# A state-space decoder layer: the first rows of running sums in two transfers, and the load of x behind the rows of step 1

## The chip, the cores and the metric

One core of a Trainium2 chip runs the whole layer in one launch. The metric is the device time of that launch in microseconds (us), the median of several runs. Five engines work side by side, each through its own list of instructions: TensorE (PE, matmuls), VectorE (DVE), ScalarE (ACT), GpSimd (POOL) and SyncE (SP, which here issues the DMA transfers). They wait for one another only by semaphores. A transfer is queued when SP issues it; the 16 DMA engines of the core carry it out.

## The reference, cut to what matters

The input x is 16 batches x 128 positions x 256 values, kept in float32. The layer is x = norm(x + mixer(x)), then x = norm(x + attention(x, ctx)), then x = norm(x + experts(x)). The change concerns only the mixer, a gated state-space mixer with 32 heads of 16 values and a state of 128. With proj = x @ W_in.T it splits into val, gate, B, C and dt, val passes a causal convolution over four positions and a silu, and per chunk of positions it computes

```python
dt = softplus(dt + dt_bias)
ld = dt * -exp(A_log)
cum = cumsum(ld)
diff = where(mask, cum[l] - cum[m], -inf)
M = (C @ B.T) * exp(diff)
Y = M @ val + C @ h * exp(cum) + D * val
out = (Y * silu(gate)) @ W_out.T
```

The reference carries a state h from chunk to chunk of 32 positions. The kernel takes all 128 positions of a batch as one chunk, for which the state at its start is zero, so that only M @ val and D * val are left.

## The kernel before, in words

`build` runs three stages one after the other: `mixer`, `attention` and `experts`. Only `mixer` is touched.

**Steps.** The mixer has 16 steps n (STEPS). The heads are cut into 4 groups of 8 heads (GROUPS), the batches into 4 blocks of 4 batches (TB blocks of NB batches, 512 tokens). Step n works on token block n % 4 and head group n // 4. Within a step there are 8 slots s, one for each head of the group. For each slot PE projects B and C (`pair`, line 789, three fp16 passes that stand for an fp32 product), ACT and DVE bring the two out of the PSUM banks as a high and a low fp16 part (`evac_b`, `evac_c` on ACT, lines 443 and 447; `low_b`, `low_c` on DVE, lines 651 and 655), PE multiplies them (`scores`, line 831), and DVE multiplies the scores by the decay exp(diff) (`weigh`, line 623). Four slots later PE applies the result to the values (`outputs`, line 843).

**The decays.** diff needs the running sums of the head along both axes. The sums lie once with tokens on the free axis, one row per head and batch (`dz`). For one axis they are turned by PE (`turn_sums`) into `cum_t`. For the other one, the rows have to stand on all 128 partitions: SP stores the sums to a scratch tensor in HBM (`store_sums`, line 192) and reads them back, broadcast to all partitions, into the tile `rows` (named cum_rows in the trace) by `load_rows` (line 197). One such load brings four heads of a group (a "quad") for four batches, 8 KB that is written to 128 partitions, 1 MB in all. `rows` has two slots, par 0 and 1, for slots 0 to 3 and 4 to 7 of a step; its layout in a partition is batch, head, position, so a batch's four heads are 2 KB in one piece. POOL then runs `exponents(n, par)`: for each of the four heads a subtraction of `cum_t` (line 286) and a causal select (line 297, `causal`), the select of head q one place behind the subtraction of head q + 1. ACT follows with `decays(n, e)`, an exp in place (line 437), and DVE with `weigh(n, e)`.

**SP's order.** SP works through its list in order: x block 0, the weight chunks, `store_sums(0, 1)` for block 0 when the sums are there, then (after the store has landed) `load_rows(0, 0, 0)`, x blocks 1 to 3 (`load_x`, tile xt_raw, shown as q_rows, 512 KB each), then a wait for `rows0`, `load_rows(0, 1, 1)`, the small dskip and the weights `wo`, a wait for the sums of all blocks, `store_sums(1, TB)`, the 2 MB of x for the residual (tile `acc`, line 212), the small `expo`, a wait for the store, and then a loop over groups with the rows of later steps. `next_rows(n, par)` waits until the slot of `rows` is free: semaphore `mixed` counts the `weigh` of DVE, and for n = 1, par = 0 it needs `weigh(0, 3)`. Each group's body has the rows of its four steps and the reload of the nine weight chunks for the next group.

**The first step.** It has an order of its own on every engine, written out by hand. PE runs `pair(0,0)` to `pair(0,3)` with `scores(0,0)` and `scores(0,1)` in between, then `step_widths(1)` and `step_widths(2)` (line 802: the dt projection of x blocks 1 and 2, each of which waits for its block of x), `scores(0,2)`, which waits for `weigh(0,0)` by the semaphore `mixed`, `turn_values(0)`, `step_widths(3)`, and then the pairs 4 to 7, each with the scores of the slot before. ACT splits the weight chunks into high parts (`hi_part`), runs `decays(0,0)` to `decays(0,2)` behind `hi_part(0,8)`, then, after PE's `step_widths(3)`, the `softplus` of blocks 1 to 3 (lines 413 to 417). DVE follows with `step_sizes`, `rates` (line 588) and three running sums (`sums`, line 569), between which `low_b(0,4)` and `low_c(0,4)` stand; `scores(0,4)` needs these. POOL runs the low parts of chunks 2 to 5 (`lo_part`, line 267), `exponents(0, 0)` with `lo_part(0, 6)` before its last select, `exponents(0, 1)` with two more low parts, `split_x(1)`, the low part of wo, `exponents(1, 0)`, `exponents(1, 1)` and so on.

**The residual.** `acc` is first used by DVE's `add_out(1, 0)` (line 646) in step 1, which waits for `in_x` at 32 (x and expo). POOL waits for the same semaphore much later, before the norm.

Of the kernel before, what the change touches and what calls it, by code (L numbers as in the profile page):

```python
# [84 lines left out]
def mixer(nc, io, acc, moments, heads):  # L85

    with ExitStack() as ctx:
# [88 lines left out]
        def _(sp):  # L176
# [23 lines left out]
            sp.wait_ge(sem("dt_cum"), 1)  # L200
            store_sums(0, 1)
            sp.wait_ge(sem("cum_out"), 16)
            load_rows(0, 0, 0)
            for t in range(1, TB):
                load_x(t)
            sp.wait_ge(sem("rows0"), 16)
# [2 lines left out]
            sp.dma_start(wo, io["wo"]).then_inc(sem("in_wo"), 16)  # L209
            sp.wait_ge(sem("dt_cum"), TB)  # L210
            store_sums(1, TB)
            sp.dma_start(acc[:], io["x"]).then_inc(sem("in_x"), 16)
            sp.dma_start(expo[:], io["expo"]).then_inc(sem("in_x"), 16)
            sp.wait_ge(sem("cum_out"), 32)

            def next_rows(n, par):
                tb, grp = n % TB, n // TB

                sp.wait_ge(sem("mixed"), 8 * n + 4 * par + 1)
                load_rows(tb, grp * 2 + par, par)  # L220
# [6 lines left out]
                        src = ctx_parts[32 * half + 8 * kv:32 * half + 8 * kv + 8, part]  # L227
                        sp.dma_start(k_rows[r:r + 8, 8 * half:8 * half + 8, :, kv, :].rearrange("d b t n -> d (b t) n"), src).then_inc(sem("k_load"), 16)

            with sp.Fori(0, GROUPS - 1) as g:  # L230
                next_rows(g * TB + 1, 0)
                next_rows(g * TB + 1, 1)
                for c in range(CHUNKS):

                    sp.wait_ge(sem("w_ready"), CHUNKS * g + c + 1)
                    sp.dma_start(w_raw[:, c].rearrange("p k n -> p (k n)"),
                                 io["w_in"][bass.ds(g + 1, 1), :, c].rearrange("g p k n -> (g p) (k n)")).then_inc(chunk_loaded(c), 16)
                with sp.Fori(2, TB + 1) as t:
                    next_rows(g * TB + t, 0)
                    next_rows(g * TB + t, 1)  # L240
            n = STEPS - TB
            sp.wait_ge(sem("w_ready"), CHUNKS * GROUPS)
            sp.dma_start(ctx_t, io["ctx_t"]).then_inc(sem("in_ctx"), 16)
# [19 lines left out]
        def _(pool):  # L263
# [16 lines left out]
            def exponents(n, par, chunks={}):  # L280

                tb, quad = n % TB, (n // TB) * 2 + par
                pool.wait_ge(sem(f"rows{par}"), 16 * n + 16)
                for q in range(4):
                    own = cum_t[:, :, bass.ds(tb * H + 4 * quad + q, 1)].broadcast_to([P, NB, L])
                    nc.gpsimd.tensor_tensor(rows[:, par, :, q], rows[:, par, :, q], own, ALU.subtract).then_inc(sem("since"), 1)  # L286
                    if q > 0:
                        causal(n, par, q - 1)
                    if q in chunks:
                        lo_part(0, chunks[q])  # L290
                causal(n, par, 3)
# [1446 lines left out]
```

## Time and profile before

| what | value |
|---|---|
| three runs | 777.16, 778.05, 782.04 us; median 778.05 |
| profiled execution, its own time | 778.42 us |
| its span | 776.5 us |
| granted TensorE clock, mean over the span | 0.982 |
| first step and what is ahead of it | up to about 46 us |
| steps 1 to 15 of the mixer | from about 46 to about 545 us |

Times in the rows are from the start of the span. A timeline row gives the start, the duration of an instruction or of several merged, the engine, the line of kernel.py, what is written and read, the count, and in brackets how long the engine was idle before it and what released it. PEld is the weight load of TensorE. Starts and ends of neighbours on PE, ACT and DVE overlap by about a tenth of a microsecond or more, since they are pipelined. SP's rows are the issues of transfers; the landing of a transfer shows in who waited for it.

### The profile page before, as it was taken

The page shows a single profiled execution, that of the slowest core. Times are in us where ns is not written, and L with a number is a line of the kernel's source. Part 1 is how long each engine was busy: PE and PEld are TensorE (multiplying, and loading weights), DVE is VectorE, ACT ScalarE, POOL GpSimd, SP SyncE. Part 2 cuts the span into 40 slices and gives each one's busy share as a digit, 9 for nine tenths or more (in the row PEclk, how much of TensorE's full clock was granted, in tenths as well). Part 3 has the DMA queues.
Part 4 walks back from the last instruction along what each step waited for, and adds up shares of the span by engine and source line. Part 5 has one row for each costly group of instructions (what it writes and reads, how often), then busy time and mean ns, then how long its engine had stood idle before and what let it go on. Part 6 is the DMA issues. An engine that isn't in the chain of part 4 may idle for free. (4 is left out here: it accounts for less than half of the span.)

```text
span 776.5 us, 17302 instructions
## 1 busy us (share of the span) xinstructions
PE 736.3 (95%) x5918; PEld 407.9 (53%) x5918; DVE 577.2 (74%) x1128; ACT 454.2 (58%) x889; POOL 352.1 (45%) x411
## 2 busy tenths in 40 slices
PE   8899999999999999999999999999689999679996
PEld 4456556565555655556555565656224443244554
DVE  5676867768676686776868679786688899838776
ACT  7754448644355754544575544646267788638775
POOL 3867535635433593333649645563023311230343
PEclk9999999999999999999999999999689999979999
DMA  6694231335224232642213324220050000000001
GB/s 208 190 232 152 55 69 47 102 54 175 62 48 107 49 59 54 175 106 49 62 54 83 106 62 92 56 55 1 15 193 23 15 23 23 14 2 1 28 28 55
DMA packets 34282, 57.91 MB, mean 75 GB/s; under 512 B 7040, under 2 KB 11904, under 8 KB 33664
## 3 DMA queue, kind: packets, MB, share of 16 engines
q1 hardware_dynamic: 33664, 57.08, 28.1%
q8 instruction: 23, 0.38, 0.2%
q10 hardware_dynamic: 576, 0.31, 0.1%
q14 instruction: 19, 0.16, 0.1%
HBM read 54.10 MB, written 2.36 MB: 73 GB/s over the span
## 5 line engine op out<-in xcount | busy, mean ns | idle before, releaser
L286 POOL TENSOR_TENSOR cum_rows<-cum_rows,cum_t 128x512 f32<-128x512 f32 x128 | 136.1, 1073 | 194.6 <-DMA cum_rows<-cum_scratch 194.6
L789 PE MATMUL pring<-xt_hi,w_hi 128*128 (+1 forms) x576 | 171.6, 380 | 0.0
L789 PE MATMUL pring<-xt_lo,w_hi 128*128 (+1 forms) x576 | 171.3, 379 | 0.0
L789 PE MATMUL pring<-xt_hi,w_lo 128*128 (+1 forms) x576 | 171.3, 379 | 0.0
L651 DVE TENSOR_TENSOR bt<-pring,bt 128x512 f16<-128x512 f32 x128 | 88.1, 688 | 71.5 <-ACT bt L443 71.5
L443 ACT CAST bt<-pring 128x512 f16<-128x512 f32 x128 | 74.6, 583 | 111.5 <-PE pring L789 111.3
L655 DVE TENSOR_TENSOR ct<-pring,ct 128x512 f16<-128x512 f32 x128 | 88.2, 689 | 53.8 <-ACT ct L447 53.5
L831 PEld LDWEIGHTS pscore<-ct,bt 128*128 128x128 f16 x1536 | 96.0, 98 | 33.8 <-issue 6.2
L831 PE MATMUL pscore<-ct,bt 128*128 128x128 f16 x1536 | 106.6, 219 | 2.8 <-issue 1.9
L447 ACT CAST ct<-pring 128x512 f16<-128x512 f32 x128 | 74.8, 585 | 52.4 <-PE pring L789 52.4
L1131 DVE TENSOR_REDUCE mx<-bank_at 128x4 f32<-128x512 f32 x128 | 83.5, 689 | 14.9 <-PE bank_at L1207 14.0
L789 PEld LDWEIGHTS pring<-xt_lo,w_hi 128*128 128x128 f16 x576 | 56.4, 98 | 68.0
L789 PEld LDWEIGHTS pring<-xt_hi,w_lo 128*128 128x128 f16 x576 | 56.4, 98 | 68.0
L623 DVE TENSOR_TENSOR mt<-pscore,cum_rows 128x512 f32<-128x512 f32 x128 | 87.1, 681 | 1.3 <-ACT cum_rows L437 1.3
L437 ACT ACTIVATE cum_rows<-cum_rows 128x512 f32<-128x512 f32 x128 | 81.2, 634 | 2.3 <-POOL cum_rows L297 2.3
L297 POOL TENSOR_SCALAR_AFFINE_SELECT cum_rows<-cum_rows 128x512 f32<-128x512 f32 x128 | 81.2, 646 | 0.0
L1093 ACT ACTIVATE probs<-bank_at 128x512 f32<-128x512 f32 x128 | 68.3, 597 | 16.7 <-PE bank_at L1216 15.1
L789 PEld LDWEIGHTS pring<-xt_hi,w_hi 128*128 128x128 f16 x576 | 50.5, 98 | 41.3 <-issue 6.5
L1046 POOL TENSOR_TENSOR acc<-acc,att 128x128 f32<-128x128 f32 (+1 forms) x32 | 14.6, 456 | 86.4 <-DVE att L1144 86.4
L1207 PE MATMUL bank_at<-k_rows,q_rows 128*128 128x512 f16 x128 | 48.4, 412 | 5.5 <-DVE mx L1131 4.0
L267 POOL TENSOR_TENSOR w_lo<-w_raw,w_hi 128x512 f16<-128x512 f32 x34 | 41.5, 1240 | 26.0 <-ACT w_raw L409 26.0
L1446 ACT ACTIVATE act_s<-bank_ex,weight 128x128 f32<-128x128 f32 x128 | 36.9, 378 | 9.2 <-PE bank_ex L1609 7.2
(153 smaller groups left out, 957.4 us busy)
## 6 DMA issues: line engine op xcount, KB each, us to landing
cum_rows<-cum_scratch SPq DMA_DIRECT2D x32, 1024.0 KB, 8.0
w_raw<-in_w_in SPq DMA_DIRECT2D x35, 256.0 KB, 6.7
q_rows<-in_xt SPq DMA_DIRECT2D x4, 512.0 KB, 11.0
acc<-in_x SPq DMA_DIRECT2D x1, 2048.0 KB, 8.5
vals<-in_vals SPq DMA_DIRECT2D x16, 128.0 KB, 2.0
out<-acc SPq DMA_DIRECT2D x8, 256.0 KB, 2.1
w_raw_e<-in_w_up SPq DMA_DIRECT2D x1, 1024.0 KB, 4.9
w_raw_e<-in_w_gate SPq DMA_DIRECT2D x1, 1024.0 KB, 6.9
```

The source lines that it names most:

```text
L286: nc.gpsimd.tensor_tensor(rows[:, par, :, q], rows[:, par, :, q], own, ALU.subtract).then_inc(sem("since"), 1)
L297: nc.gpsimd.affine_select(rows[:, par, :, q], rows[:, par, :, q], [[0, NB], [1, L]], ALU.is_ge, never, base=0, channel_multiplier=-1).then ...
L437: nc.scalar.activation(rows[:, par, :, e % 4], rows[:, par, :, e % 4], ACT.Exp).then_inc(sem("decay_exp"), 1)
L443: nc.scalar.copy(bt[:, s % 2, 0], bank[f"B{s}"][:]).then_inc(sem("b_hi"), 1)
L447: nc.scalar.copy(ct[:, s % 2, 0], bank[f"C{s}"][:]).then_inc(sem("c_hi"), 1)
L623: nc.vector.tensor_tensor(mt[:, par, s % 4].rearrange("p (b n) -> p b n", b=NB), pscore[(s + 1) % 2][:].rearrange("p (b n) -> p b n", b=NB ...
L651: nc.vector.tensor_tensor(bt[:, s % 2, 1], bank[f"B{s}"][:], bt[:, s % 2, 0], ALU.subtract).then_inc(sem("b_evac"), 1)
L655: nc.vector.tensor_tensor(ct[:, s % 2, 1], bank[f"C{s}"][:], ct[:, s % 2, 0], ALU.subtract).then_inc(sem("c_evac"), 1)
L789: mm = nc.tensor.matmul(bank[name][:], w[:, c, k, cols], x[:, k, bass.ds(n % TB, 1), :].rearrange("p o n -> p (o n)"), start=(i == 0), sto ...
L831: mm = nc.tensor.matmul(pscore[(s + 1) % 2][:, cols], bt[:, s % 2, pb, cols], ct[:, s % 2, pc, cols], start=(i == 0), stop=(i == 2))
L1093: nc.scalar.activation(probs[:, i], ring_bank("scores", 8 * b + i)[:], ACT.Exp, scale=float(8.0 ** -0.5)).then_inc(sem("probs"), 1)
L1131: nc.vector.tensor_reduce(mx[:, slot, :, i], banks[i % len(banks)][:].rearrange("p (k n) -> p k n", k=4), AX.X, ALU.max).then_inc(sem("max ...
```

## The change

The one broadcast of four heads for step 0, slot 0, becomes two broadcasts of two heads each, on the same queue one behind the other. The first raises a new semaphore, `rows_first`, the second `rows0`, which the whole one raised before. POOL waits for `rows_first` before its first subtraction and for `rows0` before its third. SP still waits for `rows0` before it issues the rows for slot 1. The load of x into `acc` and that of `expo` are moved from behind the second store of sums to behind `next_rows(1, 0)`. For that the body of the loop over groups is made a function, `load_group`, which is called once for group 0 and in the loop for groups 1 and 2.

```diff
--- before.py
+++ after.py
@@ -200,7 +200,10 @@
             sp.wait_ge(sem("dt_cum"), 1)
             store_sums(0, 1)
             sp.wait_ge(sem("cum_out"), 16)
-            load_rows(0, 0, 0)
+            for i, done in enumerate(("rows_first", "rows0")):
+                q = slice(2 * i, 2 * i + 2)
+                sp.dma_start(rows[:, 0, :, q].rearrange("p b q n -> p b (q n)"),
+                             cum_d[0].rearrange("(b h) n -> b h n", h=H)[:, q, :].rearrange("b q n -> b (q n)").partition_broadcast(P)).then_inc(sem(done), 16)
             for t in range(1, TB):
                 load_x(t)
             sp.wait_ge(sem("rows0"), 16)
@@ -209,8 +212,6 @@
             sp.dma_start(wo, io["wo"]).then_inc(sem("in_wo"), 16)
             sp.wait_ge(sem("dt_cum"), TB)
             store_sums(1, TB)
-            sp.dma_start(acc[:], io["x"]).then_inc(sem("in_x"), 16)
-            sp.dma_start(expo[:], io["expo"]).then_inc(sem("in_x"), 16)
             sp.wait_ge(sem("cum_out"), 32)
 
             def next_rows(n, par):
@@ -227,8 +228,8 @@
                         src = ctx_parts[32 * half + 8 * kv:32 * half + 8 * kv + 8, part]
                         sp.dma_start(k_rows[r:r + 8, 8 * half:8 * half + 8, :, kv, :].rearrange("d b t n -> d (b t) n"), src).then_inc(sem("k_load"), 16)
 
-            with sp.Fori(0, GROUPS - 1) as g:
-                next_rows(g * TB + 1, 0)
+            def load_group(g):
+
                 next_rows(g * TB + 1, 1)
                 for c in range(CHUNKS):
 
@@ -238,6 +239,14 @@
                 with sp.Fori(2, TB + 1) as t:
                     next_rows(g * TB + t, 0)
                     next_rows(g * TB + t, 1)
+
+            next_rows(1, 0)
+            sp.dma_start(acc[:], io["x"]).then_inc(sem("in_x"), 16)
+            sp.dma_start(expo[:], io["expo"]).then_inc(sem("in_x"), 16)
+            load_group(0)
+            with sp.Fori(1, GROUPS - 1) as g:
+                next_rows(g * TB + 1, 0)
+                load_group(g)
             n = STEPS - TB
             sp.wait_ge(sem("w_ready"), CHUNKS * GROUPS)
             sp.dma_start(ctx_t, io["ctx_t"]).then_inc(sem("in_ctx"), 16)
@@ -280,8 +289,11 @@
             def exponents(n, par, chunks={}):
 
                 tb, quad = n % TB, (n // TB) * 2 + par
-                pool.wait_ge(sem(f"rows{par}"), 16 * n + 16)
+                first = isinstance(n, int) and n + par == 0
+                pool.wait_ge(sem("rows_first" if first else f"rows{par}"), 16 * n + 16)
                 for q in range(4):
+                    if first and q == 2:
+                        pool.wait_ge(sem("rows0"), 16)
                     own = cum_t[:, :, bass.ds(tb * H + 4 * quad + q, 1)].broadcast_to([P, NB, L])
                     nc.gpsimd.tensor_tensor(rows[:, par, :, q], rows[:, par, :, q], own, ALU.subtract).then_inc(sem("since"), 1)
                     if q > 0:
```

## Rows read from the trace of the kernel before

**Rows 1.** Page, part 1: busy us, share of the span and instructions of each engine.

```profile
...
PE 736.3 (95%) x5918; PEld 407.9 (53%) x5918; DVE 577.2 (74%) x1128; ACT 454.2 (58%) x889; POOL 352.1 (45%) x411
...
```

**Rows 2.** Windows view, core 0: busy us by engine, granted clock, DMA share, GB/s.

```profile
...
60.00:545.00 485.00, 481.70 (x4256) 283.07 (x4253) 359.04 (x584) 258.64 (x458) 257.74 (x295) 1.00 0.31 76
...
```

**Rows 3.** Timeline of TensorE: start us, us, engine line op out<-in xcount [idle before <-releaser].

```profile
...
24.64 0.64 PE L802 MATMUL py<-q_rows,wdt 128*32 128x128 f32 x16 [1.30 <-DMA q_rows<-in_xt]
26.12 0.83 PE L831 MATMUL pscore<-ct,bt 128*128 128x128 f16 x12 [0.83 <-DVE mt L623]
...
27.32 0.64 PE L802 MATMUL py<-q_rows,wdt 128*32 128x128 f32 x16
...
35.24 0.83 PE L831 MATMUL pscore<-ct,bt 128*128 128x128 f16 x12 [1.32 <-issue]
...
57.30 0.69 PEld L831 LDWEIGHTS pscore<-ct,bt 128*128 128x128 f16 x12 [0.46 <-issue]
...
```

**Rows 4.** Timeline of ScalarE, 20 to 30 us.

```profile
...
24.56 0.63 ACT L437 ACTIVATE cum_rows<-cum_rows 128x512 f32<-128x512 f32 x1
...
27.16 0.63 ACT L437 ACTIVATE cum_rows<-cum_rows 128x512 f32<-128x512 f32 x1 [0.97 <-POOL cum_rows L297]
28.03 0.58 ACT L413 ACTIVATE q_rows<-py,dtb 128x384 f32<-128x384 f32 x1 [0.24 <-PE py L802]
...
```

**Rows 5.** Timeline of VectorE, 20 to 62 us.

```profile
...
25.28 0.69 DVE L623 TENSOR_TENSOR mt<-pscore,cum_rows 128x512 f32<-128x512 f32 x1 [0.93 <-ACT cum_rows L437]
...
31.04 1.51 DVE L588 SCALAR_TENSOR_TENSOR q_rows<-q_rows,rate 128x384 f32<-128x384 f32 x1 [1.28 <-ACT q_rows L417]
...
34.48 0.66 DVE L655 TENSOR_TENSOR ct<-pring,ct 128x512 f16<-128x512 f32 x1
...
55.09 1.53 DVE L682 SCALAR_TENSOR_TENSOR val_t<-th_val,conv_h 128x512 f32<-128x512 f32 x1
...
60.56 1.27 DVE L646 TENSOR_TENSOR acc<-pring,acc 128x512 f32 x2
...
```

**Rows 6.** Timeline of GpSimd, 18 to 57 us.

```profile
...
18.06 1.16 POOL L267 TENSOR_TENSOR w_lo<-w_raw,w_hi 128x512 f16<-128x512 f32 x1 [0.85 <-ACT w_raw L409]
21.28 2.05 POOL L286 TENSOR_TENSOR cum_rows<-cum_rows,cum_t 128x512 f32<-128x512 f32 x2 [2.06 <-DMA cum_rows<-cum_scratch]
23.29 0.64 POOL L297 TENSOR_SCALAR_AFFINE_SELECT cum_rows<-cum_rows 128x512 f32<-128x512 f32 x1
...
30.09 2.05 POOL L286 TENSOR_TENSOR cum_rows<-cum_rows,cum_t 128x512 f32<-128x512 f32 x2 [1.24 <-DMA cum_rows<-cum_scratch]
...
50.36 2.06 POOL L286 TENSOR_TENSOR cum_rows<-cum_rows,cum_t 128x512 f32<-128x512 f32 x2 [5.65 <-DMA cum_rows<-cum_scratch]
...
55.03 1.04 POOL L286 TENSOR_TENSOR cum_rows<-cum_rows,cum_t 128x512 f32<-128x512 f32 x1
...
```

**Rows 7.** Source view of line 682: duration ns min/median/max, first and last start.

```profile
...
L682 DVE SCALAR_TENSOR_TENSOR val_t<-th_val,conv_h x16: 676/682/1533, 15.2 to 514.6; 128x512 f32<-128x512 f32 x16
...
```

**Rows 8.** Timeline of the DMA issues on SyncE, 10 to 49 us.

```profile
...
10.22 0.35 SPq L192 DMA_DIRECT2D cum_scratch<-q_rows  x1
11.77 0.39 SPq L197 DMA_DIRECT2D cum_rows<-cum_scratch  x1
...
21.16 0.39 SPq L197 DMA_DIRECT2D cum_rows<-cum_scratch  x1
...
36.15 1.53 SPq L212 DMA_DIRECT2D acc<-in_x  x1
...
39.09 9.58 SPq L197 DMA_DIRECT2D cum_rows<-cum_scratch  x2
...
```

**Rows 9.** Windows view, 12 to 22 us, columns as in rows 2.

```profile
...
12.00:20.00 8.00, 8.00 (x57) 4.39 (x55) 5.86 (x10) 6.95 (x14) 3.48 (x3) 1.00 0.68 138
20.00:22.00 2.00, 2.00 (x14) 0.94 (x12) 0.69 (x1) 1.67 (x5) 0.72 (x1) 1.00 0.99 385
...
```

**Rows 10.** Page, part 6: DMA issues, KB each, median us to landing.

```profile
...
cum_rows<-cum_scratch SPq DMA_DIRECT2D x32, 1024.0 KB, 8.0
...
```

## The prediction

> **What bounds the kernel now.** I read the page's busy table first. TensorE (PE) is busy for 736.3 of 776.5 us [rows 1]; the other engines are far below. The windows view then says where the missing 40 us are not: from 60 to 545 us, the whole steady part of the mixer, PE is busy for 481.7 of 485 us [rows 2]. The change touches only what runs before 60 us, so it can win only what PE waits there, and what it wins or loses is carried to the end as a constant shift, since behind it PE has no slack to absorb it. The span is 776.5 us and the profiled execution took 778.42 us; the sum below is made against the latter, which lies 0.4 us over the median 778.05 of the three runs.
>
> The PE timeline of the first step has these waits [rows 3]: 1.30 us at 24.64 for the third block of x (`step_widths(2)`), 0.83 us at 26.12 for `weigh(0,0)`, 1.32 us at 35.24 before `scores(0,4)`, and in step 1 a gap of 0.46 us at 57.30 before `scores(1,1)`. Together 3.9 us, 0.5% of the kernel: no better order of these transfers can win more. For each I asked who is late, in the timelines of the other engines.
>
> - 26.12: PE waits for `weigh(0,0)` on DVE (25.28), and DVE waited 0.93 us for ACT [rows 5]. ACT ran `decays(0,0)` at 24.56, directly behind `hi_part(0,8)`, with no idle time before it [rows 4]. Its input from POOL, the first causal select, was ready at 23.29 + 0.64 = 23.93 [rows 6]. So ACT's queue is late here, by 0.6 us, not POOL and not the rows.
> - 35.24: `scores(0,4)` needs `low_c(0,4)`, which DVE ran at 34.48 to 35.14. DVE is busy back to `rates` at 31.04, which waited 1.28 us for ACT's logarithm and then itself took 1.51 us [rows 5]. ACT's part of that chain starts at 28.03, on PE's `step_widths(3)` at 27.32 [rows 3, 4]. That block of PE stands behind `scores(0,2)`, so behind the first point.
> - 57.30: `scores(1,1)` waits for the DVE chain of step 1, in which `val_silu` at 55.09 took 1.53 us; the median of its 16 executions is 0.68 [rows 5, 7].
>
> **Part 1, the first rows in two halves.** Now the whole megabyte is issued at 11.77, and has landed when SP issues the next one at 21.16, 9.4 us later [rows 8]. POOL finished `lo_part(0,5)` at 18.06 + 1.16 = 19.22, idled 2.06 us and began `exponents(0,0)` at 21.28 [rows 6]. With halves, the first lands at about 11.77 + 4.7 = 16.5, if bytes set the time; the extra issue costs SP 0.4 us (11.77 to 12.21) and only pushes the issue of x, which queues behind the rows anyway. POOL then starts at 19.22, 2.06 us earlier. It does two subtractions (2.05) and one select (0.64) and reaches the new wait for the second half at 21.9; the second half, landing as the megabyte did, is there at 21.2. Behind that new wait stand the third subtraction and all the rest of POOL's program, `lo_part(0,6)` first; none waits. `exponents(0,0)` ends 2.06 us earlier.
>
> Who profits? `decays(0,0)`: nobody, since ACT gets to it at 24.56 whatever POOL does. `decays(0,2)` at 27.16 waited 0.97 us for POOL and now comes about 1.4 us earlier, but ACT's next item, at 28.03, waits for PE's `step_widths(3)` [rows 4], which is unmoved. On POOL, the next item is `exponents(0,1)`, which already waited 1.24 us for its rows and began at 30.09 [rows 6]; those rows are issued only when `rows0` is complete, 21.16 as before, so POOL stands idle 3.3 us instead of 1.24. PE's two waits at 24.64 and 26.12 stay: the third block of x is queued behind the same bytes. I take 0 for part 1.
>
> Bounds for its unknown, the landing of the second half. The trace has no broadcast in 1 KB pieces; the old one is 512 pieces of 2 KB, the new ones 1,024 of 1 KB. Between 12 and 20 us, with the rows in front of the queue, the DMA engines moved 138 GB/s at a share of 0.68; between 20 and 22, with x on them, 385 GB/s at 0.99 [rows 9]. So a broadcast out of 8 KB of memory is slow already, and not by bytes through the engines. If each piece costs the same time whatever its size, the second half lands 8 us later, at 29.2. At the other end the halves go as fast as x: then it could land at up to 5 us earlier, and the third block of x with it; PE would win back its 1.30 us at 24.64 but still wait for ACT until about 26.1, so below nothing is worth 0. I take bytes as the measure, since both broadcast and x pieces are far larger than what the small transfers of this kernel use, and because the limit looks like one of the source, which is the same. Delays up to 0.84 us are free (PE's second wait covers a later x); above that each microsecond costs PE one.
>
> One rule of the Trainium skill speaks against the split. "DMA: Bandwidth & Descriptors", section Bandwidth, says to batch into transfers of 1 MiB or more, and its section on the anatomy of a DMA gives a fixed part of about 2.0 us for each. Where two transfers are queued one behind the other the trace shows otherwise: three transfers of 512 KB each follow one another at 385 GB/s.
>
> **Part 2, x behind the rows of step 1.** Now x (2 MB) is issued at 36.15 and the rows of step 1, first half, at 39.09, behind it [rows 8]; POOL idled 5.65 us and began at 50.36 [rows 6]. Afterwards these rows are the first in the queue. Their issue still waits for the store of the sums, so 39.09 at the latest; at the median of 8.0 us from issue to landing [rows 10] they are there at 47.1, and POOL starts 3.3 us earlier. `exponents(1,0)` is four subtractions of 1.04 and four selects of 0.64, 6.7 us, and ends at 53.8 instead of 57.1 or later.
>
> PE does not wait for POOL in step 1, so the direct gain is 0. An indirect one is in the rows: `val_silu` began at 55.09 while POOL's subtraction of 55.03 + 1.04 ran, and ended at 56.62, 0.55 after that one's end [rows 5, 6]. The same stands at 31.04, where `rates` ended 0.41 us after POOL's pair of 30.09 + 2.05. Such an operation, with both inputs in SBUF, seems held until POOL lets go. With POOL done at 53.8, `val_silu` takes 0.68 [rows 7], the chain loses 0.85 us, and PE's gap of 0.46 at 57.30 goes. Bounds: 0 if the rows land after 48.4 (then POOL still runs at 55.09), and 0.85, all that `val_silu` loses. I take the gap, 0.5. The Trainium skill has this as a rule, "SBUF — State Buffer", Who interferes with whom: VectorE and GpSimd share one pair of ports, and the second to issue waits for the whole instruction of the first; the trace agrees, with 1.53 against 0.68 us.
>
> What is late next: x itself. It now lands behind a megabyte more, at 47.1 + 8.5 = 55.6 at the latest, and its first use is `add_out(1,0)` at 60.56 [rows 5]: covered by 5 us; without cover each microsecond would be PE's, through the ring banks. The second rows of step 1 are issued when `weigh(1,-1)` is done, about 48.3, and find 2 MB ahead of them; but the sum of bytes is the same, the queue only starts its big transfer some 2 to 3 us later, so they land 1 to 3 us later than now; their first use is `decays(1,4)`, two slots of the step behind `add_out(1,0)`. The weights of group 1, which are queued next, are used three steps later. The loop body taken out for group 0 issues the same DMAs; I cost it at nothing, since SP only waits there.
>
> **Sum.** 778.42 + 0 - 0.5 = 777.9; from the median, 777.6.
>
> **Rivals.**
> 1. *The second half lands late.* For: the broadcast runs at 138 GB/s, far from the 385 of x, and half of the source addresses serve each half. Against: the engines' share of 0.68 leaves room for more pieces. It decides from 0.84 us of delay on; then x's third block holds PE at 24.64 one for one, and the rows for `exponents(0,1)`, issued when the second half is there, follow. At 4 us: 777.6 + 3.2 = 780.8. At 8 us: 784.8. Slower than before.
> 2. *Each transfer pays its fixed time in series.* The smallest bound from the rows is the 64 KB store of sums, issued at 10.22 and landed at 11.77, 1.55 us [rows 8]. A delay of 1.55 us, less 0.84, gives 777.6 + 0.7 = 778.3. Against it stand the x blocks at full rate. With the page's 2.0 us, which no run here shows, an estimate would be 778.8.
> 3. *POOL's new phase frees `rates`.* `rates` at 31.04 lost about 1 us to POOL's pair begun at 30.09. If the rows of `exponents(0,1)` land only a little later, or POOL's second subtraction starts behind the DVE operation, that microsecond goes, and PE's 1.32 us at 35.24 shrinks by it: 777.6 - 1.0 = 776.6. For: only about 0.1 us decide who goes first (31.04 against 30.09 + 1.04). Against: nothing in the change moves it on purpose.
> 4. *Nothing of it reaches PE*, part 2's half microsecond either, as the rows land after 48.4: 778.1. This is also the case in which the change does what it says and is without use.
>
> **Chances.** Forecast 0.40, rival 4 0.20, rival 3 0.17, rival 1 0.15 (most of it below 781), rival 2 0.08. A measurement of this kernel can tell about 1% (7.8 us) from no change. Faster by more is nearly excluded, since PE waits only 3.9 us where the change acts: 0.01. Slower by more needs rival 1 at its upper end and something besides: 0.02. The rest, 0.97, is no change that can be told. The range is 775.8 to 780.8: below, rival 3 with 0.8 us for the spread of the runs; above, rival 1 at 4 us.
>
> **What would show it.** Right: POOL's `exponents(0,0)` begins near 19.2 and its wait before `exponents(0,1)` grows from 1.24 to about 3.3 us; `decays(0,0)` still at about 24.5 and `scores(0,2)` at about 26.1; `exponents(1,0)` begins near 47; `val_silu` of step 1 takes 0.68 and the gap at 57.30 is gone; PE's instructions from step 2 on are 0.5 us earlier. Wrong: a second wait of POOL inside `exponents(0,0)`, SP's next rows issued well behind 22, `step_widths(2)` later than 24.64 (rival 1 or 2); `rates` at 0.5 us instead of 1.51 (rival 3); `add_out(1,0)` waiting for x.

## The result and the profile after

The change makes the kernel slower by 0.6%: the changed one has a median of 781.45 us (22 runs), the one before 776.88 us (22 runs beside them), ratio 1.0061 with a 95% interval of 1.0045 to 1.0076. The forecast was 777.6 us, and its range ended at 780.8. Ratios and intervals here and below leave out slow executions, those over 1.5% above the fastest of their kernel; only the padded changed kernel further down had any, two of twelve.

The two profiled executions hardly show this as a sum: their spans are 776.7 us after and 776.5 before. The stage that the change touches does. The last `low_y` of the mixer began at 545.16 us before and at 549.75 after, 4.6 us later, which is about the difference of the medians. What took it back in this one execution lies behind the mixer, where the clock is granted differently from execution to execution: between 650 and 700 us TensorE had 0.90 of full speed before and 0.97 after. So all that follows is read at marks inside the mixer. They carry a few tenths of spread of their own: TensorE began its last matmuls ahead of x block 1, where the change had not yet reached it, at 22.48 us after and at 22.18 before.

First SyncE's issues, which answer to [rows 8]:

```profile
...
10.73 0.35 SPq L192 DMA_DIRECT2D cum_scratch<-q_rows  x1
12.29 0.94 SPq L205 DMA_DIRECT2D cum_rows<-cum_scratch  x2
13.26 5.28 SPq L181 DMA_DIRECT2D q_rows<-in_xt  x3
26.96 0.39 SPq L197 DMA_DIRECT2D cum_rows<-cum_scratch  x1
...
41.28 0.40 SPq L192 DMA_DIRECT2D cum_scratch<-q_rows  x1
44.31 0.39 SPq L197 DMA_DIRECT2D cum_rows<-cum_scratch  x1
44.74 0.51 SPq L244 DMA_DIRECT2D acc<-in_x  x1
...
```

The two halves are issued at 12.29, and the next rows, which wait for the second half, at 26.96: 14.7 us, where the whole megabyte took 9.4. TensorE's timeline, against [rows 3]:

```profile
...
28.20 1.08 PE L814 MATMUL py<-q_rows,wdt 128*32 128x128 f32 x16 [5.12 <-DMA q_rows<-in_xt]
30.31 1.08 PE L814 MATMUL py<-q_rows,wdt 128*32 128x128 f32 x16 [1.03 <-DMA q_rows<-in_xt]
31.33 1.46 PE L843 MATMUL pscore<-ct,bt 128*128 128x128 f16 x12
...
33.36 0.64 PE L814 MATMUL py<-q_rows,wdt 128*32 128x128 f32 x16
...
40.81 0.83 PE L843 MATMUL pscore<-ct,bt 128*128 128x128 f16 x12 [0.85 <-issue]
```

TensorE waits 5.12 us for x block 1, which stands in the queue behind both halves and for which its matmuls had not waited before; `step_widths(2)` comes 5.7 us later and `scores(0,2)` 5.2 us. After the wait it also runs slowly for a while: `scores(0,2)` takes 1.46 us instead of 0.83. The windows view has the clock; its last three columns are the granted clock as a share of full speed, the busy share of the DMA engines, and GB/s:

```profile
...
12.00:20.00 8.00, 7.32 (x49) 3.79 (x48) 6.23 (x11) 7.02 (x15) 3.60 (x4) 1.00 0.66 91
20.00:22.00 2.00, 2.00 (x17) 1.11 (x15) 0.69 (x1) 1.67 (x4) 1.75 (x2) 1.00 0.82 127
20.00:27.00 7.00, 3.08 (x21) 1.41 (x18) 2.77 (x4) 5.16 (x10) 2.65 (x3) 0.95 0.81 174
27.00:32.00 5.00, 2.77 (x39) 1.87 (x40) 0.69 (x1) 1.26 (x2) 4.95 (x6) 0.50 0.97 272
...
```

From 27 to 32 us the granted clock is 0.50, the lower of the two levels, 1.2 GHz. It fell shortly after 26 us, while TensorE stood still, and was back by about 33. And the engines moved 91 GB/s from 12 to 20 us, against 138 before, and 127 instead of 385 from 20 to 22 [rows 9].

GpSimd, against [rows 6]:

```profile
...
20.25 2.05 POOL L298 TENSOR_TENSOR cum_rows<-cum_rows,cum_t 128x512 f32<-128x512 f32 x2 [0.72 <-DMA cum_rows<-cum_scratch]
...
27.01 1.05 POOL L298 TENSOR_TENSOR cum_rows<-cum_rows,cum_t 128x512 f32<-128x512 f32 x1 [4.11 <-DMA cum_rows<-cum_scratch]
...
35.48 2.23 POOL L298 TENSOR_TENSOR cum_rows<-cum_rows,cum_t 128x512 f32<-128x512 f32 x2 [3.51 <-DMA cum_rows<-cum_scratch]
...
```

The first half lands at 20.25, one microsecond before the whole did, and GpSimd begins that much sooner; then it waits 4.11 us inside `exponents(0,0)` for the second half, and 3.51 for the rows of `exponents(0,1)`. ScalarE follows:

```profile
...
24.87 0.62 ACT L449 ACTIVATE cum_rows<-cum_rows 128x512 f32<-128x512 f32 x1
28.68 0.63 ACT L449 ACTIVATE cum_rows<-cum_rows 128x512 f32<-128x512 f32 x1 [3.19 <-POOL cum_rows L309]
30.28 0.63 ACT L449 ACTIVATE cum_rows<-cum_rows 128x512 f32<-128x512 f32 x1 [0.97 <-POOL cum_rows L309]
34.07 0.58 ACT L425 ACTIVATE q_rows<-py,dtb 128x384 f32<-128x384 f32 x1 [3.15 <-PE py L814]
...
```

`decays(0,0)` stays where it was, behind `hi_part(0,8)`, as forecast; `decays(0,1)` now waits 3.19 us.

### The profile page after: what moved, and what is told of

Its sections match the earlier page's. It is cut to its first block and busy times, and to the rows that moved or that the text cites. A ratio compares the mean times of both kernels' runs of the same rounds, so it can differ in the third digit from the quotient of the medians.

```text
span 776.7 us, 17261 instructions
## 1 busy us (share of the span) xinstructions
PE 732.9 (94%) x5910; PEld 406.3 (52%) x5918; DVE 575.4 (74%) x1128; ACT 453.8 (58%) x889; POOL 352.4 (45%) x411
```

## The experiments

The theories changed on the way; the expectations show how. Marks in the mixer for all of them stand in a table at the end of this section.

**The two parts alone.** The first has the split, with x for the residual left where it was:

```diff
             store_sums(1, TB)
+            sp.dma_start(acc[:], io["x"]).then_inc(sem("in_x"), 16)
+            sp.dma_start(expo[:], io["expo"]).then_inc(sem("in_x"), 16)
...
             next_rows(1, 0)
-            sp.dma_start(acc[:], io["x"]).then_inc(sem("in_x"), 16)
-            sp.dma_start(expo[:], io["expo"]).then_inc(sem("in_x"), 16)
             load_group(0)
```

> Only the split of the first rows; x for the residual stays where the kernel before has it. If the split alone makes the loss: the second half lands some 6 us later than the whole megabyte did, SP issues the next rows near 27 instead of 21.2, TensorE waits about 5 us for the x block of step_widths(1), and the time is 4 to 6 us above the kernel before, ratio about 1.006. If moving x makes it: 778 or so, ratio 1.000.

Measured: 782.17 us beside 776.96, ratio 1.0064 (1.0042 to 1.0085), the whole loss. The second half landed at 27.24.

The second has the move alone:

```diff
-            for i, done in enumerate(("rows_first", "rows0")):
-                q = slice(2 * i, 2 * i + 2)
-                sp.dma_start(...).then_inc(sem(done), 16)
+            load_rows(0, 0, 0)
...
-                pool.wait_ge(sem("rows_first" if first else f"rows{par}"), 16 * n + 16)
+                pool.wait_ge(sem(f"rows{par}"), 16 * n + 16)
```

> Only the move of x; the first rows come in one transfer. My prediction for this part alone: exponents(1,0) begins near 47 instead of 50.4, val_silu of step 1 takes 0.7 us, TensorE's gap before scores(1,1) goes, and the time is 0.5 us below the kernel before, ratio 0.999. The rival, that x or the second rows of step 1 come too late: add_out(1,0) waits, ratio above 1.002.

Measured: 776.49 us beside 776.96, ratio 0.999 (0.9967 to 1.0013). The size is the forecast one, but the interval holds 1 as well. The mixer's end mark moved by 0.5 us, to 544.64. The timelines of GpSimd and VectorE in step 1:

```profile
...
49.68 2.05 POOL L292 TENSOR_TENSOR cum_rows<-cum_rows,cum_t 128x512 f32<-128x512 f32 x2 [4.68 <-DMA cum_rows<-cum_scratch]
...
```

```profile
...
54.99 0.94 DVE L688 SCALAR_TENSOR_TENSOR val_t<-th_val,conv_h 128x512 f32<-128x512 f32 x1
...
56.45 1.10 DVE L645 TENSOR_TENSOR y_parts<-skip,y_parts 128x512 f16<-128x512 f32 x1
...
```

GpSimd begins at 49.68, not near 47: the rows were issued at 39.18 and took 10.5 us, with 2 MB of x right behind them in the queue. `val_silu` takes 0.94 us, not 0.68, and `low_y` still 1.10. The gap of TensorE's loads at 57.30 is gone. But the next experiment, which leaves x where it was, shows the same: there GpSimd begins at 49.83, `val_silu` takes 0.93 us, the gap is gone too, and the end mark is 0.4 us earlier. So the half microsecond is not shown to come from the move: one execution without it differs from another by as much. Nothing of step 1 waited for x: `add_out(1,0)` ran at 59.87 without a wait, and the second rows of the step came 2.5 us later (61.07 instead of 58.52), within the forecast 1 to 3.

**Is it the number of pieces, the source, or the transfer?** Two transfers again, but by batch, so that the pieces stay 2 KB:

```diff
-            load_rows(0, 0, 0)
+            for b in range(0, NB, 2):
+                sp.dma_start(rows[:, 0, b:b + 2].rearrange("p b q n -> p b (q n)"),
+                             cum_d[0].rearrange("(b h) n -> b h n", h=H)[b:b + 2, 0:4, :].rearrange("b q n -> b (q n)").partition_broadcast(P)).then_inc(sem("rows_first" if b == 0 else "rows0"), 16)
```

> The first rows in two transfers of two batches each, all four heads: the pieces stay 2 KB, 256 of them per transfer, but each transfer reads only half of the source (4 KB). GpSimd waits for both. Theory A, the broadcast's time goes by the number of pieces: each half takes about 4 us, both have landed about 9.5 us after the first issue, SP's next rows are issued as in the kernel before. Theory B, it goes by how many source addresses are read at once: each half takes as long as the whole, and the next rows are issued some 14 to 15 us after the first issue. Theory D, each transfer pays a fixed time: 1.5 to 2 us later than before.

Measured: issued at 12.01, the next rows at 21.52, so 9.5 us for both: a transfer more costs next to nothing, and half of the source per transfer neither. This spoke for theory A, the number of pieces. Its rows of step 1, on GpSimd and VectorE, for the comparison above:

```profile
...
49.83 2.06 POOL L290 TENSOR_TENSOR cum_rows<-cum_rows,cum_t 128x512 f32<-128x512 f32 x2 [4.72 <-DMA cum_rows<-cum_scratch]
...
```

```profile
...
55.15 0.93 DVE L686 SCALAR_TENSOR_TENSOR val_t<-th_val,conv_h 128x512 f32<-128x512 f32 x1
...
```

Then all loads from a scratch tensor in which a load's source is one piece of 8 KB:

```diff
-        cum_d = nc.dram_tensor("cum_scratch", (TB, NB * H, L), F32, kind="Internal").ap()
+        cum_d = nc.dram_tensor("cum_scratch", (TB, H, NB, L), F32, kind="Internal").ap()
...
-        rows = sb("cum_rows", [P, 2, NB, 4, L], F32)
+        rows = sb("cum_rows", [P, 2, 4, NB, L], F32)
...
+                for b in range(NB):
+                    sp.dma_start(cum_d[t0:t1, :, b].rearrange("t h n -> h t n"),
+                                 dz[b * H:b * H + H, 0, t0 * L:t1 * L].rearrange("h (t n) -> h t n", n=L)).then_inc(sem("cum_out"), 16)
```

> The scratch tensor is laid out by block, head, batch, position, so that the source of one load is 8 KB in one piece, and the slots of the rows tile go head, batch, position to match. All 32 loads are then 128 pieces of 8 KB. The stores of the sums become four transfers each, one per batch. Theory A: a quarter of the pieces, so a load takes 3 to 4 us from issue to landing (near the full rate of 1 MB in 2.7 us) instead of 8. Theory B: the source is as small as before, 8 us. Theory C, the 16 KB stride between the four pieces of one load is what is slow: 3 to 4 us, as theory A. If loads are fast, the x block for step_widths(2) comes early, TensorE loses its 1.3 us there, and the time is 1 to 2 us below the kernel before; the 1.1 us for three more issues of stores stands against it.

Measured: 4.8 us from issue to landing as the median of 32 loads, instead of 8.0 [rows 10]. The time did not fall: 778.79 us, ratio 1.0026 (0.9997 to 1.0054). Why is in TensorE's timeline of the first step:

```profile
...
23.20 1.08 PE L802 MATMUL py<-q_rows,wdt 128*32 128x128 f32 x32
26.61 0.83 PE L831 MATMUL pscore<-ct,bt 128*128 128x128 f16 x12 [2.33 <-DVE mt L623]
...
35.08 0.83 PE L831 MATMUL pscore<-ct,bt 128*128 128x128 f16 x12 [0.67 <-issue]
37.03 1.08 PE L843 MATMUL py<-mt,val_pad 128*32 128x128 f32 x32 [1.12 <-issue]
...
```

TensorE no longer waits for x at 24.64, and waits 2.33 us for `weigh(0,0)` instead: ScalarE's order is the limit there, as the prediction had read it. Then two waits, of 0.67 and 1.12 us, come where one of 1.32 and one of 0.40 had been (the 0.40 in front of `outputs(0,0)` at 36.48). Steps 2 to 15 took 467.7 us instead of 465.8, with TensorE waiting five times for `low_y` on VectorE, 1.3 us in all.

Theories A and C (the 16 KB between the pieces of one load) both had a faster load here, though with 3 to 4 us and not 4.8. Pieces of 2 KB and of 1 KB, each in one transfer, out of nearly packed sources, tell them apart. Of the first, then of the second:

```diff
-        cum_d = nc.dram_tensor("cum_scratch", (TB, H, NB, L), F32, kind="Internal").ap()
+        cum_d = nc.dram_tensor("cum_scratch", (TB, H, NB * L + 64), F32, kind="Internal").ap()
```

> As the kernel with the packed scratch tensor, but 256 bytes of padding behind every 2 KB, so that one load is again 512 pieces of 2 KB, read from four neighbouring places instead of four that lie 16 KB apart. Theory A (number of pieces): 8 us from issue to landing, as in the kernel before. Theory C (the 16 KB stride was slow): 4.8 us, as with the packed scratch.

```diff
-        cum_d = nc.dram_tensor("cum_scratch", (TB, H, NB, L), F32, kind="Internal").ap()
+        cum_d = nc.dram_tensor("cum_scratch", (TB, 2 * H, 2 * L + 64), F32, kind="Internal").ap()
```

> The same with 256 bytes of padding behind every 1 KB: each load is one transfer of 1,024 pieces of 1 KB. Theory A: the time doubles against pieces of 2 KB, 14 to 16 us from issue to landing, for every load of the mixer; then the rows come slower than the steps use them and the kernel becomes much slower. If only the split into two transfers were slow, and not the small pieces: 8 us.

From the pages of the two, part 6 and the count of packets; first 2 KB, then 1 KB:

```profile
...
DMA packets 34378, 57.92 MB, mean 75 GB/s; under 512 B 7136, under 2 KB 12000, under 8 KB 33760
...
cum_rows<-cum_scratch SPq DMA_DIRECT2D x32, 1024.0 KB, 5.5
...
```

```profile
...
DMA packets 50762, 57.92 MB, mean 75 GB/s; under 512 B 7136, under 2 KB 44768, under 8 KB 50144
...
cum_rows<-cum_scratch SPq DMA_DIRECT2D x32, 1024.0 KB, 5.6
...
```

5.5 and 5.6 us. Twice the pieces, all else alike, make no difference: theory A is out, which I had held after the two runs before. That left the addresses. In the kernel before, the four 2 KB pieces of a load lie 16 KB apart; in the changed one four pieces of 1 KB lie 16 KB apart. Taken modulo 16 KB, a load reads a band of 2 KB, a half one of 1 KB, the loads by batch 2 KB, the packed ones 8 KB or more. The rates follow: 8 us for 1 MB from a band of 2 KB, 6.7 and 8.0 us for 512 KB from 1 KB, 9.5 us for two times 512 KB from 2 KB, 4.8 to 5.6 us for 1 MB from 8 KB or more. I called this theory E. The 16 KB in it is not measured: taken modulo 4 or 8 KB, the loads fall in the same order.

**Theory E, tried three ways.** Padding behind each batch in the scratch tensor changes only the distance between the pieces, and makes four stores of the sums out of one. The changed kernel with 1 KB (the others have 512 and 4096 in place of 256):

```diff
-        cum_d = nc.dram_tensor("cum_scratch", (TB, NB * H, L), F32, kind="Internal").ap()
+        cum_d = nc.dram_tensor("cum_scratch", (TB, NB, H * L + 256), F32, kind="Internal").ap()
...
+                for b in range(NB):
+                    sp.dma_start(cum_d[t0:t1, b, 0:H * L].rearrange("t (h n) -> h t n", n=L),
+                                 dz[b * H:b * H + H, 0, t0 * L:t1 * L].rearrange("h (t n) -> h t n", n=L)).then_inc(sem("cum_out"), 16)
```

> The changed kernel, with 1 KB of padding in the scratch tensor behind each batch: the four pieces that a load reads lie 17 KB apart instead of 16. Theory E, formed from the runs so far: the rate of a broadcast goes by the width of the source's address band modulo 16 KB (2 KB for a whole load, 1 KB for a half, 8 KB with the packed source), not by the number of pieces. Then a half has a band of 4 KB, takes less than 4 us instead of 7 to 8, SP issues the next rows near 20 instead of 27, TensorE's 5 us for x go, and the time is within 1 us of the kernel before or below: ratio 0.997 to 1.001. If small pieces are slow with a stride of any such size: ratio 1.005 as the changed kernel.

```profile
...
10.33 1.75 SPq L193 DMA_DIRECT2D cum_scratch<-q_rows  x4
13.16 0.96 SPq L206 DMA_DIRECT2D cum_rows<-cum_scratch  x2
14.16 1.64 SPq L181 DMA_DIRECT2D q_rows<-in_xt  x3
19.35 0.39 SPq L198 DMA_DIRECT2D cum_rows<-cum_scratch  x1
...
```

Both halves, 1,024 pieces of 1 KB, land 6.2 us after the issue instead of 14.7, and the time is 776.63 us beside 776.96, ratio 1.0003 (0.9973 to 1.0034). The pieces are as many and as small as in the changed kernel and land in the same places of SBUF. So the loss is cured by 1 KB of padding, with the split left in. And with the loss gone the split wins nothing: TensorE's waits in the first step are 2.33, 0.67 and 1.12 us, and in the kernel before with 2 KB of padding, which follows, they are 2.33, 0.67 and 1.11 without a split. (Both also have four stores of the sums in place of one, and all their loads are faster.) The kernel before with 2 KB of padding, and its control with 16 KB:

> The kernel before, with 2 KB of padding behind each batch: stride 18 KB, band 8 KB, pieces and their number unchanged (512 of 2 KB). Theory E: a load takes 5.5 us from issue to landing, as with the packed source in pieces of 2 KB, instead of 8.0.

> Its control: 16 KB of padding behind each batch, stride 32 KB, so that the band modulo 16 KB is 2 KB again; the four stores are those of the 18 KB kernel. Theory E: 8.0 us, as in the kernel before. If padding of any size, or the four stores, made the loads fast: 5.5 us.

Part 6 of the two pages, 18 KB first, then 32 KB:

```profile
...
cum_rows<-cum_scratch SPq DMA_DIRECT2D x32, 1024.0 KB, 4.9
...
```

```profile
...
cum_rows<-cum_scratch SPq DMA_DIRECT2D x32, 1024.0 KB, 8.1
...
```

4.9 us at 18 KB and 8.1 at 32 KB, with the same stores, the same number and size of pieces. It is the distance, 16 or 32 KB against 17 or 18, and neither padding as such nor the stores. That 16 and 32 KB come out alike fits the band and not the bare distance. As a cure for the kernel before it won nothing that one execution could show: the mixer's end mark is 545.49 with 2 KB of padding.

**What the late half holds up.** The changed kernel with x blocks 1 and 2 between the two halves:

```diff
                 sp.dma_start(rows[:, 0, :, q]...).then_inc(sem(done), 16)
-            for t in range(1, TB):
-                load_x(t)
+                for t in ((1, 2), (3,))[i]:
+                    load_x(t)
```

> The changed kernel, with the x blocks 1 and 2 issued between the two halves of the first rows, block 3 behind them. If the loss runs only through the x blocks that TensorE waits for, it is gone: ratio 1.000. If the late second half holds GpSimd, ScalarE and so the softplus as well, the 5 us come back there: TensorE has no wait for x near 23, but waits before scores(0,4); ratio 1.005 to 1.008.

Measured: 780.06 us, ratio 1.0042 (1.0021 to 1.0063). TensorE's timeline:

```profile
...
24.73 0.65 PE L814 MATMUL py<-q_rows,wdt 128*32 128x128 f32 x16 [1.39 <-DMA q_rows<-in_xt]
26.02 0.83 PE L843 MATMUL pscore<-ct,bt 128*128 128x128 f16 x12 [0.65 <-DVE mt L635]
...
28.67 1.08 PE L814 MATMUL py<-q_rows,wdt 128*32 128x128 f32 x16 [1.02 <-DMA q_rows<-in_xt]
...
34.21 0.83 PE L843 MATMUL pscore<-ct,bt 128*128 128x128 f16 x12
...
40.09 0.59 PE L801 MATMUL pring<-xt_hi,w_hi 128*128 128x512 f16 x2 [0.78 <-POOL w_lo L276]
...
44.42 0.59 PE L801 MATMUL pring<-xt_hi,w_hi 128*128 128x512 f16 x2 [0.90 <-POOL w_lo L276]
...
```

The 5.12 us near 23 is gone, `scores(0,2)` is at 26.02 as in the kernel before, and yet most of the loss is back. TensorE waits 1.02 us for x block 3, and 0.78 and 0.90 us for the low parts `lo_part(0,7)` and `lo_part(0,8)`, which stand behind the rows in GpSimd's order; before `scores(0,4)`, where I had expected the wait, there is none. A late second half holds two things, x and low parts, and taking one away shows the other.

The three waits, 2.7 us, are not the whole account. The clock is granted at 0.50 from 27 to 32 us here too. `scores(0,3)` comes at 34.21, and in the kernel before at this place:

```profile
...
30.50 0.83 PE L831 MATMUL pscore<-ct,bt 128*128 128x128 f16 x12
...
```

That is 3.7 us, of which about 2.4 are work at the low clock (5.54 us from `step_widths(3)` to `scores(0,3)` instead of 3.18). Part of it only fills the 1.32 and 0.40 us that TensorE waited before at `scores(0,4)` and `outputs(0,0)`, so what the clock costs in the end is not separated. Nor can it be put down to the late half: the run by batch had 0.50 from 27 to 30 us as well, with its rows in time, and its mixer ended no later for it. TensorE was as busy here from 22 to 27 us (2.95 us) as in the kernel before (2.87), whose clock stayed at 1.00. What sets it off is open.

**A version that beats both.** First x moved, the first rows from a packed scratch tensor of their own in one transfer, all later rows in pieces of 2 KB out of the padded scratch tensor of the experiment above, and ScalarE's `decays(0,0)` ahead of `hi_part(0,8)`. A cut of the edit, against the kernel before:

```diff
+        first_d = nc.dram_tensor("first_scratch", (H, NB, L), F32, kind="Internal").ap()
...
-            load_rows(0, 0, 0)
+            first_rows(0)
...
+                decays(0, 0)
                 hi_part(0, 8, True)
-                for e in range(3):
+                for e in range(1, 3):
                     decays(0, e)
```

> A version meant to beat both: x moved behind the rows of step 1; the rows of step 0 come from a packed scratch tensor of their own (128 pieces of 8 KB, one transfer), the rows of all later steps in pieces of 2 KB, so that GpSimd works in the later steps when it did before; and ScalarE runs decays(0,0) ahead of hi_part(0,8), since the rows are no longer late and ScalarE's order is what TensorE waits for at 26 us. Expected: decays(0,0) near 23.5, scores(0,2) near 25.2, 1 us sooner than in the kernel before, and with the 0.5 us of the moved x a time 1 to 1.5 us below it, ratio 0.998. If the four stores in place of one cost as much as they did with the packed scratch alone: ratio 1.000.

Measured: 775.55 beside 776.82 us, ratio 0.9993 (0.9966 to 1.0019), so no gain that can be told. `scores(0,2)` came at 25.56, and then VectorE lost what it had won:

```profile
...
30.48 1.02 DVE L603 SCALAR_TENSOR_TENSOR q_rows<-q_rows,rate 128x384 f32<-128x384 f32 x1 [1.02 <-ACT q_rows L431]
31.53 1.15 DVE L584 TENSOR_TENSOR_SCAN q_rows<-q_rows 128x128 f32<-128x128 f32 x1
...
33.18 1.22 DVE L584 TENSOR_TENSOR_SCAN q_rows<-q_rows 128x128 f32<-128x128 f32 x1
...
34.91 1.33 DVE L584 TENSOR_TENSOR_SCAN q_rows<-q_rows 128x128 f32<-128x128 f32 x1
...
```

The running sums (line 584) take 1.15, 1.22 and 1.33 us. GpSimd, no longer late, works through that whole stretch. So I let it wait for the last sum behind the first select of `exponents(0,1)`, with the low parts of chunks 7 and 8 right behind that wait:

```diff
                     if q in chunks:
-                        lo_part(0, chunks[q])
+                        if par == 1:
+                            pool.wait_ge(sem("dt_cum"), TB)
+                        for c in chunks[q]:
+                            lo_part(0, c)
...
-            exponents(0, 1, {1: 7, 3: 8})
+            exponents(0, 1, {1: (7, 8)})
```

> The version with the packed first rows, in which GpSimd waits for the last of VectorE's running sums behind the first select of exponents(0,1), and runs the low parts of chunks 7 and 8 right after that. Theory: the 0.5 us won at scores(0,2) was given back since GpSimd, no longer late, held VectorE's rates and sums (1.0 to 1.3 us each instead of 0.4 to 0.6); with GpSimd idle there, scores(0,4) starts near 33.4 instead of 35.1 and outputs(0,0) near 34.6 instead of 37.0, and the mixer is about 2.3 us shorter: ratio 0.996 to 0.997. If the late low parts or exponents of the step then hold TensorE: no gain, ratio 0.999 or above.

```profile
...
30.24 0.62 DVE L606 SCALAR_TENSOR_TENSOR q_rows<-q_rows,rate 128x384 f32<-128x384 f32 x1 [1.00 <-ACT q_rows L434]
30.89 0.42 DVE L587 TENSOR_TENSOR_SCAN q_rows<-q_rows 128x128 f32<-128x128 f32 x1
...
31.82 0.41 DVE L587 TENSOR_TENSOR_SCAN q_rows<-q_rows 128x128 f32<-128x128 f32 x1
...
32.73 0.41 DVE L587 TENSOR_TENSOR_SCAN q_rows<-q_rows 128x128 f32<-128x128 f32 x1
...
```

```profile
...
32.96 0.83 PE L849 MATMUL pscore<-ct,bt 128*128 128x128 f16 x12
34.11 1.08 PE L861 MATMUL py<-mt,val_pad 128*32 128x128 f32 x32 [0.32 <-issue]
...
```

The sums take 0.41 to 0.42 us each, with GpSimd idle from 29.74 to 33.23; `scores(0,4)` runs at 32.96 without a wait and `outputs(0,0)` at 34.11. The time is 774.00 us beside 776.96, ratio 0.996 (0.9943 to 0.9977): better than the kernel before and than the changed one. An added wait made it faster. (The low part of chunk 8 moved forward with it; that the sums are short when GpSimd is idle, the run with x between the halves shows as well: 0.42, 0.41 and 0.62 us, with GpSimd idle from 32.43 to 36.02 and the first two starting at 34.93 and 35.85.)

The marks, from VectorE's timelines: start of the first convolution of step 2, and of the last `low_y` of the mixer.

| kernel | step 2, us | end of mixer, us | load, median us |
|---|---|---|---|
| before | 79.32 | 545.16 | 8.0 |
| after | 84.38 | 549.75 | 8.0, halves 11.0 |
| split alone | 85.01 | 550.80 | 8.2, halves 11.4 |
| x moved alone | 79.07 | 544.64 | 8.1 |
| two by batch | 79.19 | 544.76 | 8.1, halves 7.4 |
| packed, 8 KB pieces | 79.37 | 547.09 | 4.8 |
| 2 KB pieces | 81.81 | 547.18 | 5.5 |
| 1 KB pieces | 80.02 | 545.39 | 5.6 |
| x between the halves | 82.67 | 548.50 | 8.0, halves 11.6 |
| after, stride 17 KB | 79.71 | 545.37 | 5.4, halves 4.7 |
| before, stride 18 KB | 79.40 | 545.49 | 4.9 |
| before, stride 32 KB | 81.73 | 547.51 | 8.1 |
| first rows packed | 79.37 | 544.86 | 5.6, first 6.3 |
| the same, GpSimd waits | 77.10 | 542.57 | 5.5, first 6.2 |

Each mark is of one execution. Five kernels (by batch, 2 KB and 1 KB pieces, 18 and 32 KB) have only that one, so their marks say less than their loads; in the one with 2 KB pieces the granted clock was 0.91 from 30 to 50 us, where it was 1.00 before.

## Why the prediction was wrong, point by point

**The step that failed** is the choice in part 1, "I take bytes as the measure", with its reason "because the limit looks like one of the source, which is the same". The limit is one of the source, but a half does not read the same source: it reads half the band of addresses, at about two thirds of the rate. The rows after the second half were issued 14.7 us after the first issue, not 9.4. The term was set to 0 and measured +5 (the split alone, 782.17 beside 776.96). That a whole load is slow at 16 or 32 KB between its pieces and the halves fast at 17 is shown; the band as the reason fits every load here but was not varied by itself. The prediction had this case as rival 1, with half of the source addresses per half named as what speaks for it, and gave it 0.15. The upper bound, 8 us later for the second half, came from the idea that each piece costs its own time. The measured 5.3 us lie inside it, but the reason was wrong: one transfer in pieces of 1 KB ran at 5.6 us.

**The price of rival 1** came out. A delay of 5.3 us less the cover of 0.84 is 4.5; less the forecast's 0.5 for x, and from the larger sample's 776.88, that is 780.9, and 781.45 was measured. The place was one instruction earlier than said: TensorE waited already at x block 1 (22.70 before), since all three blocks stand behind both halves. The price did not have the low clock from 27 to 32 us: `step_widths(2)` took 1.08 us instead of 0.64, and from `scores(0,2)` to `step_widths(3)` it was 2.03 us instead of 1.20, together 1.3. On the other side, `rates` took 1.04 us instead of 1.51 and TensorE's wait before `scores(0,4)` shrank from 1.32 to 0.85, which is rival 3 as a side effect. With both the sum would be 781.7, so that the price came as near as it did partly because these two, neither of them in it, work against each other.

**"Who profits?"**, answered with nobody, held. The changed kernel at a stride of 17 KB has the split without its penalty; its ratio to the kernel before is 1.0003 (0.9973 to 1.0034), and TensorE waits in it as in the unsplit kernel at 18 KB. ScalarE reached `decays(0,0)` behind `hi_part(0,8)` in every run that left its order alone.

**"Behind that new wait stand ... `lo_part(0,6)` first; none waits"** supposed the second half on time. In the changed kernel no wait for a low part shows, since TensorE was late itself. With x between the halves, it waited 1.7 us for low parts that GpSimd had not got to.

**Rival 2**, a fixed time for each transfer in series, is out: two transfers by batch took 9.5 us against 9.4. The rule of the Trainium skill on batches, "DMA: Bandwidth & Descriptors", Bandwidth, would have pointed to the right side and for a reason that no run here bears out (its figures are of transfers issued from GpSimd; here SyncE issues them). Closer is a row of the same page's section Latency and other measured facts, on row pitches at large powers of two in HBM: it tells of copies whose rows lie 2 or 4 MiB apart and which fall to as little as half the rate, and of 4 KiB of padding that bring it back. I had not weighed it, as the pitch here is 16 KB. The padding works here too, with 8.0 us at 16 KB against 4.9 at 18.

**Part 2** is not borne out, though x moved alone measured a time 0.5 us lower. The rows landed at 49.68 instead of 47.1, behind the prediction's own bound of 48.4, from which on it expected nothing (rival 4), and `val_silu` still ran beside GpSimd. The kernel by batch lost the same gap of TensorE at 57.30 without the move, so that the agreement with -0.5 may be luck. The rows took 10.5 us from issue to landing against a median of 8; that the 2 MB queued right behind them slow them is a reading that no run tried.

**The range** ended at the price of a 4 us delay, though the case that the bound allowed went to 8. That cut had no row behind it.

## What to carry to other kernels

Before a transfer is cut in parts, look at which addresses each part reads at once, not only at its bytes: a broadcast from four places 16 KB apart took 14.7 us instead of 9.4 when it was cut so that each transfer read half of each place, and a kilobyte of padding in the scratch tensor brought the two halves down to 6.2. A late transfer costs at each thing queued behind it, data and waits, so price all of them. A gain of half a microsecond in one execution, with its mechanism plain in the rows, can still be the spread of the executions: look for it in a run that leaves the change out. And where an engine that shares the SBUF with another is made earlier, ask what it now runs beside: here the gain came only when GpSimd was told to wait.

## What the runs showed of the hardware that I had not expected

- A broadcast of 1 MB to 128 partitions from HBM takes 8.0 to 8.2 us when its four source pieces lie 16 or 32 KB apart, and 4.8 to 5.6 us when they lie 17 KB, 18 KB, 2.25 KB or nothing apart or are eight of 1 KB that lie 1.25 KB apart (medians over a kernel's loads). Which part of the memory makes this was not tried.
- GpSimd and VectorE hold each other up in more operations than the two the prediction named: a running sum of 128x128 took 0.41 to 0.42 us with GpSimd idle and 1.15 to 1.33 beside it.
- One kernel with faster loads for every step was slower in the later ones: with packed 8 KB pieces, steps 2 to 15 took 467.7 us, with the loads before 465.8. That GpSimd's work then falls on VectorE's `low_y`, for which TensorE waited five times, is read from one trace; the loads at a stride of 18 KB are as fast and took only 466.1, so this stays open.
- The clock fell to 0.50 from about 26 or 27 us on, for 3 to 10 us, in the changed kernel and both others with the late half, and for some 3 us in the ones by batch and with 1 KB pieces, where the rows were in time. In the one with 2 KB pieces it fell near 38 us. In the kernel before and the seven others it stayed at 1.00 from 24 to 38 us. No run here shows what decides it.
